# In a three-layer GRU stage, ScalarE normalises a finished group one step later and TensorE turns its rows behind two gate products

## The reference

```
x = x + L1_gnn(layernorm(x), adj)            # the block of the change
    for i in range(3):
        aggr = A^T @ (h @ weight[i])         # A = (adj != 0)
        r = sigmoid(i_r + h_r);  z = sigmoid(i_z + h_z)
        n = tanh(i_n + r * h_n)
        h = (1 - z) * n + z * h
x = x + L1_ffn(layernorm(x), ...)            # its norm, gate scores and top 2
                                             # are made in the same stage
```

## Time and profile before

| what | us |
|---|---|
| three runs, median (lowest to highest) | 1134.66 (1134.47 to 1137.16) |
| the profiled execution, its own time | 1134.32 |
| its span | 1132.6 |
| the GRU stage's turns 1 to 7 (545 to 850) | 305 |

### The profile page before, as it was taken

How to read it: one execution, slowest core, us unless ns; L and a number is a source line. 1 busy time by engine, 2 the same in 40 slices (tenths; PEclk the granted TensorE clock), 3 DMA queues, 4 the chain that set the end, 5 groups by cost and what they waited for, 6 DMA issues and landing times. The chain is left out here.

```text
span 1132.6 us, 27053 instructions
## 1 busy us (share of the span) xinstructions
PE 977.3 (86%) x6816; PEld 802.3 (71%) x6817; DVE 766.8 (68%) x2985; ACT 578.4 (51%) x1469; POOL 601.0 (53%) x622
## 2 busy tenths in 40 slices
PE   4677776699999999859999999999985899999980
PEld 3666665499999999825555555555553789999980
DVE  3666666476666666437788888888975555555548
ACT  3777776333434343225555665565553334444455
POOL 2277777475555555510135554545545677767670
PEclk8777877699999999959999999999996899999995
DMA  9511111242222222130230321303010634333349
GB/s 229 201 49 47 49 47 54 71 115 78 70 67 72 69 69 69 41 124 0 75 89 24 96 69 54 101 29 121 25 42 31 130 107 112 93 91 90 90 143 365
DMA packets 109669, 99.08 MB, mean 87 GB/s; under 512 B 33424, under 2 KB 94480, under 8 KB 109328
## 3 DMA queue, kind: packets, MB, share of 16 engines
q1 hardware_dynamic: 92432, 62.83, 20.7%
q0 software_dynamic: 17152, 35.29, 9.3%
HBM read 55.44 MB, written 42.62 MB: 87 GB/s over the span
## 5 line engine op out<-in xcount | busy, mean ns | idle before, releaser
L1680 POOL DMA_INDIRECT result<-e_y,e_ids x280 | 280.2, 1001 | 164.2 <-issue 80.6
L415 POOL DMA_INDIRECT queue<-rows,slots x256 | 263.7, 1030 | 173.1 <-issue 121.2
L1711 PE MATMUL e_ps_h<-e_xT,e_up_of 128*128 128x128 f32 x2240 | 277.2, 278 | 3.0 <-DVE e_hT L1824 2.8
L1711 PEld LDWEIGHTS e_ps_h<-e_xT,e_up_of 128*128 128x128 f32 x2240 | 264.9, 194 | 4.0 <-issue 3.0
L1726 PE MATMUL e_ps_y<-w_sb,e_hT 128*128 x1664 | 208.3, 275 | 0.0
L1726 PEld LDWEIGHTS e_ps_y<-w_sb,e_hT 128*128 128x128 f32 x1664 | 196.8, 192 | 0.2 <-issue 0.2
L1750 ACT ACTIVATE e_hT<-e_ps_h,b_sb 128x128 f32<-128x128 f32 x272 | 77.9, 368 | 112.7 <-PE e_ps_h L1711 112.7
L1781 DVE COPY e_up_of<-w_sb 128x512 f32 x280 | 112.4, 441 | 4.1 <-issue 0.4
L1809 DVE TENSOR_SCALAR e_hT<-e_ps_h,b_sb 128x128 f32<-128x128 f32 x272 | 76.4, 343 | 32.8 <-PE e_ps_h L1711 32.6
L1824 DVE TENSOR_TENSOR e_hT<-e_ps_h,e_gate 128x512 f32<-128x512 f32 x72 | 49.7, 690 | 71.1 <-ACT e_gate L1759 71.0
L1759 ACT ACTIVATE e_gate<-e_ps_h 128x512 f32<-128x512 f32 x72 | 43.0, 597 | 96.8 <-PE e_ps_h L1711 95.5
(11 more groups left out here) (217 smaller groups left out, 1783.5 us busy)
## 6 DMA issues: line engine op xcount, KB each, us to landing
xq<-queue SPq DMA_DIRECT2D x280, 64.5 KB
g_y<-result SPq DMA_DIRECT2D x20, 512.0 KB, 4.0
result<-e_y,e_ids POOLq DMA_INDIRECT x280, 2.3
x_res<-x SPq DMA_DIRECT2D x16, 256.0 KB, 3.8
w_sb<-w SPq DMA_DIRECT2D x2, 2048.0 KB, 12.0
queue<-rows,slots POOLq DMA_INDIRECT x256, 2.5
w_sb<-w SPq DMA_DIRECT2D x16, 256.0 KB
rows<-result SPq DMA_DIRECT2D x8, 512.0 KB, 8.2
```

What stands on the lines that cost most here:

```text
L415: pool.indirect_dma_start(out=queue, out_offset=bass.IndirectOffsetOnAxis(ap=c.slots[q][:, k, t:t + 1], axis=0), in_=c.rows[q][:, k, t, :] ...
L1680: pool.indirect_dma_start(out=result, out_offset=bass.IndirectOffsetOnAxis(ap=ids[at_down.k][:, t, :].bitcast(U32), axis=0), in_=y[at_down ...
L1711: last = pe.matmul(ps_h[b][:, t, q * P:(q + 1) * P], up_of[at_up.k % 4][:, t, q * P:(q + 1) * P], xT[at_up.k % 4][:, t, :], start=True, st ...
```

## The change

ScalarE's `norm_tail(pa[0])`, a wait and four activations, moves from the end of step k = 1, where it stood ahead of `gate_r` of (0,1), to step k = 2, between `gate_z` of (0,1) and `agg_out` of (1,0). `norm_tail(pa[1])` stays where it is, in step k = 2 behind `tail_rows(pa[0])`. On TensorE the call `inside()` of a layer above 0, which is `first_turn` alone, moves from ahead of the state's two gate products to behind them. No instruction is added, removed or altered.

```diff
@@ TensorE, run(n, l, b, inside)
                 if l == 0:
                     wait(pe, AH, "state", at.s)
                     pe.matmul(ps_hn[b][:], c.w_hh[:, 2 * D:3 * D], h[:], start=True, stop=True)
-                if inside:
+                if inside and l == 0:
                     inside()
                 after(pe, s_z, u, 1)
                 pe.matmul(ps_r[:], c.w_hh[:, 0:D], h[:], start=True, stop=False)
                 pe.matmul(ps_z[:], c.w_hh[:, D:2 * D], h[:], start=True, stop=False)
+                if inside and l:
+                    inside()
                 after(pe, s_aggT, u)
@@ ScalarE, body(n, ...)
                     if k == 5 and has_head and has_run:
                         head(nx[0])
+                    if k == 2 and has_tail:
+                        norm_tail(pa[0])
                     if has_run:
                         agg_out(n, l, b)
@@
                     if k in (2, 3) and has_tail:
                         tail_rows(pa[k - 2])
-                    if k in (1, 2) and has_tail:
-                        norm_tail(pa[k - 1])
+                    if k == 2 and has_tail:
+                        norm_tail(pa[1])
```

## The result

The changed kernel takes 1126.60 us (median of six runs, 1124.80 to 1127.91), the kernel before 1135.73 beside it on the same chip (six runs, 1134.47 to 1137.16). The ratio is 0.9919, with an interval of 0.9906 to 0.9932: faster by 7.7 to 10.7 us. The forecast was 1129.0 and its range ended at 1126.8. The sign was right; the gain was larger than forecast, and the time came 0.2 us outside the range.

What follows compares the result with a forecast made beforehand. The prediction took TensorE to set the GRU stage's turn; gains of 1.40 (turns 1, 2), 3.12 (turns 3 to 6) and 1.03 (turn 7) sum to 5.55 us off 1134.32, giving 1129.0 us after the median's 0.34, range 1126.8 to 1131.8.

Steps and rivals of the forecast that it cites:

- Part 1: Moving norm_tail(pa[0]) away from ahead of the sigmoid of r lets the aggregation start earlier, gaining 1.12 us a turn.
- Part 2: norm_tail placed ahead of agg on ScalarE delays agg to 646.01, at zero cost to TensorE, with 0.4 us cover.
- Part 3: First group's row turn behind the two gate products: rows come 0.2 us in time; worth nothing alone, carries Part 1.
- What is late next: Second group's rows come only 0.71 us earlier, so TensorE stalls 0.34 before their turn and keeps 0.78 of 1.12.
- The sum: GRU turns 1 and 2 gain 0.70 each, turns 3 to 6 0.78 each, turn 7 1.03: together 5.55 us.
- The upper bound: A turn of the GRU stage can gain no more than 1.12 us, all of the aggregation's wait for tok.
- A: No second stall before the second group's row turn, all gain kept: 7.6 us, 1127.1; chance 0.10.
- margin of 0.1: Second group's norm_tail ends at 651.65, before its row turn loads at 651.77: 0.1 us taken as spare.
- B: Covers for the moved row turn or agg are thinner: 1.8 to 3.7 us left, 1130.6 to 1132.5; chance 0.15.
- C: Another engine bounds and TensorE's time is given back later in the turn: no change, 1134.0 to 1134.6; chance 0.07.
- D: Moved norm_tail starts late, waiting for GpSimd's shift, and holds agg and TensorE every turn: 1138 or more; chance 0.04.

Runs made afterwards that it cites:

- the extra wait: Kernel before, with VectorE starting the new state in step (0,1) only after GpSimd's second-group power: 1133.13 us, ratio 0.9988.
- the variant that waits for the shift: Changed kernel with turn 7's second-group ranks and probabilities behind step (2,1), plus VectorE's new state in step (0,1) waiting for GpSimd's power and shift: 1123.72 us, ratio 0.9892.
- the extra instruction: Changed kernel plus one unused two-SBUF-input VectorE tensor_tensor a turn, behind the second group's statistics in step (0,1): 1126.01 us, ratio 0.9920.
- the control: Changed kernel plus the same unused VectorE tensor_tensor a turn, placed behind the new state of step (0,1), away from GpSimd's power: 1127.37 us, ratio 0.9934.

## Why the prediction was right and where it failed

- **Part 1: right.** L1241 starts 0.86 behind L1237, not 1.98: 1.12 gained. That ScalarE's half alone and TensorE's half alone gain nothing agrees with the text on part 3, "worth nothing alone and carries part 1".
- **Part 2: right.** `norm_tail` starts 0.57 behind the sigmoid of z (643.09 to 643.66) and `agg` 1.94 behind the aggregation, forecast about 2.0. TensorE does not wait for it: the first product with `agg` starts 3.14 behind the aggregation, as the 3.15 of the earlier trace rows had it.
- **Part 3: right.** The rows end at 645.30 (643.66 + 1.64), and their turn's first load is at 645.54 without a wait.
- **"What is late next": wrong,** and this is the step that failed. It put the second group's chain 0.71 earlier and let TensorE stall 0.34; the chain came 1.20 earlier and of the stall 0.02 is there. Three numbers in it were off, and they are the failed step in its own terms. First, the candidate comes 0.83 earlier (1.91 behind L1235 before, 1.08 after), not 0.71: I let it start 0.05 behind the end of the residual add, but it starts 0.60 behind that add's start, while the add still has 0.08 to go. Second, the power takes 1.04, not 1.52, and the shift 0.65, not 0.53: 0.36 more. I had taken GpSimd's durations as fixed, though they hang on what VectorE does beside them, which the change moves. Third, the "margin of 0.1", which was a wait of 0.1 (below); the 0.05 that I gave the handover from the rows to the load is 0.12 in my own rows. With most of that wait gone too, the gain of a turn is 0.08 or 0.09 more than the 1.12.
- **"The sum": each turn's term mis-sized** by that step: 0.70, 0.78 and 1.03 stood for 1.04 and 1.01 (turns 1, 2), 1.20 (turns 3 to 6) and 1.22 (turn 7). 5.55 forecast, 8.1 measured. In turns 1 and 2 the wait of L1241 was worth 1.00 and not 1.12 (L1241 started 1.86 behind L1237). A turn lasts 43.60, not 44.0. The upper bound, "no more than 1.12", failed by the same 0.1.
- **The rivals.** A (no second stall, 7.6 us) came nearest, and "GpSimd's queue or VectorE's add could also come earlier" named the place without the mechanism. I gave it 0.10 for the sake of that margin. B is refuted by the covers, which held. C is refuted by the turn: VectorE, busy 40.50 of 45 us in the stretch after, went along, and the whole gain reached the stage's end. D did not occur; the shift stood ready.

**The wait read as a margin.** Ahead of the second row turn TensorE makes eight score products, and the distance from their start to the row turn's shows whether it was held. In the kernel before (timeline of turn 3):

```profile
650.88 0.96 PE L1281 MATMUL g_ps_q<-gate_w_sb,g_rT 128*128 128x16 f32 x8
...
651.80 0.63 PE L1275 MATMUL g_ps_m<-ident,rows 128*128 128x128 f32 x4
```

That is 0.92. Where the rows are ready early it is 0.81: in the kernel before with the extra wait (649.26 to 650.07, above), and so it is in all seven turns there, with ScalarE's half alone, and in the variant that waits for the shift. So the products were held by 0.1 in turns 3 to 7 (0.90 to 0.92 there, 0.81 to 0.84 in turns 1 and 2), though the view of waits lists nothing.

**How near it still is.** In the kernel after:

```profile
648.98 0.96 PE L1283 MATMUL g_ps_q<-gate_w_sb,g_rT 128*128 128x16 f32 x8
...
649.81 0.63 PE L1277 MATMUL g_ps_m<-ident,rows 128*128 128x128 f32 x4
```

It is 0.83, so 0.02 of the wait is left. The rows end at 649.66 (648.01 + 1.65), 0.11 ahead of the load, which is the same handover as before, and there is no margin: with 0.23 more in the chain the turn grew by 0.22, and with 0.4 less in it (the variant that waits for the shift) it shrank by at most 0.02.

## What to carry to other kernels

When a wait goes, the next one is where two chains meet with almost no distance: compare there the distance between the starts of neighbouring products with the same distance where the data came early (here 0.92 with 0.81), since a "margin" as short as a handover may be a wait. Do not carry durations of a small instruction over to the new order as they stand: look at what ran beside it in each case of the old order, the odd ones too (here the last turn's 1.04 among fourteen of 1.5). And judge an effect of 0.2 us a turn by the turn's length in the trace, which repeats to 0.02, not by the total.

## What the runs showed of the hardware

**GpSimd and VectorE.** In these traces a small GpSimd instruction that starts while VectorE runs an instruction with two operands in SBUF is held until about that one's end. The shift shows it best. Its timeline in the kernel before (the shift itself is in the earlier trace rows):

```profile
649.14 0.69 DVE L1460 TENSOR_TENSOR g_state<-g_rg,g_new 128x512 f32<-128x512 f32 x1
```

And in the last turn of the kernel after, with no such VectorE instruction beside it:

```profile
859.37 0.20 POOL L270 TENSOR_TENSOR g_tail_shift<-g_tail_minus_mean,g_tail_rstd 128x4 f32<-128x4 f32 x1
```

The shift takes 0.20 alone. With VectorE beside it, it ends 0.05 to 0.06 behind VectorE's end, whenever that is: at 649.89 for 649.83 before, at 647.94 for 647.89 where VectorE waits for the power. The power ends 0.90 behind VectorE's end when held (649.28 for 648.37, and 646.05 for 645.15 with the extra instruction) and takes 1.04 alone. The hold needs both of VectorE's operands in SBUF, as far as these traces show: with VectorE's residual add beside it, which reads one of its two from PSUM (`g_ps_m`), the power was not held. In the last turn of the control (the extra instruction later in the step):

```profile
857.26 0.68 DVE L1493 TENSOR_TENSOR x_res<-g_ps_m,x_res 128x512 f32<-128x512 f32 x1
857.34 1.04 POOL L268 TENSOR_TENSOR g_tail_rstd<-g_tail_vare,half_neg 128x4 f32<-128x4 f32 x1 [2.67 <-DVE g_tail_vare L261]
```

The Trainium skill ("SBUF — State Buffer", section "Who interferes with whom") states that a VectorE instruction with two SBUF inputs contends with a GpSimd instruction that reads SBUF; the traces agree, with 0.44 to 0.49 us more for each power. The Trainium skill ("SBUF — State Buffer", section "SBUF: two separate sides") says that whichever of the two starts first holds the shared ports for the whole instruction. The rows show that in one direction only: in the kernel after, VectorE's instruction starts at 646.42 in the midst of the power (646.13 to 647.17) and takes its usual 0.69. The most that one took beside a shift that started with it was 0.73 (at 559.99, turn 1 of the kernel after).

**TensorE's clock.** After the wait of 2.72 us that ended at 841.97 in the kernel after, the mean granted clock was 0.64 of full speed (2.4 GHz) over 844 to 848, so most of that stretch ran at the lower level, 1.2 GHz; without that wait it stayed at 1.00 there. In the kernel before it fell too, behind the same wait, which ended at 848.79. Busy time by stretch before:

```profile
848.00:852.00 4.00, 3.21 (x22) 2.17 (x23) 1.37 (x9) 1.18 (x2) 1.29 (x2) 0.62 0.26 67
```

But with TensorE's half alone the same wait of 2.72 us, which ended there at 845.46, was followed by this:

```profile
844.00:848.00 4.00, 2.54 (x27) 1.92 (x28) 2.00 (x10) 1.18 (x2) 0.96 (x1) 1.00 0.28 66
848.00:852.00 4.00, 4.00 (x13) 1.85 (x12) 2.34 (x6) 1.39 (x4) 2.34 (x2) 1.00 0.15 50
```

From the state turn of step (1,1) in turn 7 to the stage's end that kernel takes 47.1 us, the kernel before 48.6: 1.5 less, which is about what the drop cost beyond the wait. (Its whole stage is 3.0 shorter, 383.50 and not 386.46; the other 1.4 lies at the stage's start, where its clock rose earlier: 0.80 over 498 to 502, and 0.50 in the kernel before.) The same wait stands in nine of the traces, and the clock fell behind it in eight. So such a wait can cost more than its length, and does not always. What decides, no run here shows.
